# A transformer decoder layer on one core: one table for all eight PSUM banks, and new places for the attention work

## What is computed

```
x = x + attn(layernorm(x))            # self-attention, full 512x512 scores, with biases
x = x + xattn(layernorm(x), ctx_512)  # cross-attention, keys and values from a latent of 128, causal mask
x = x + ffn(layernorm(x))             # 512 -> 2048, exact gelu, -> 512, with biases

scores = einsum('bhsd,bhtd->bhst', q, k) * scale
p = exp(scores - max(scores));  out = (p @ v) / sum(p)
```

## Time and profile before

| | |
|---|---|
| time of the 3 runs, us | 1168.91 (1166.37 to 1170.12) |
| span of the profiled execution, us | 1169.0 |
| mean granted clock of TensorE | 0.996 |
| TensorE busy, us (share) | 1127.7 (96%) |
| TensorE weight loads busy, us | 767.5 (66%) |
| VectorE busy, us | 686.7 (59%) |
| ScalarE busy, us | 485.9 (42%) |
| GpSimd busy, us | 432.9 (37%) |

### The profile page before, as it was taken

How to read it: one execution, slowest core, us unless ns; L and a number is a source line. 1 busy time by engine, 2 the same in 40 slices (tenths; PEclk the granted TensorE clock), 3 DMA queues, 4 the chain that set the end, 5 groups by cost and what they waited for, 6 DMA issues and landing times.

```text
span 1169.0 us, 15851 instructions
## 1 busy us (share of the span) xinstructions
PE 1127.7 (96%) x5840; PEld 767.5 (66%) x5840; DVE 686.7 (59%) x1302; ACT 485.9 (42%) x792; POOL 432.9 (37%) x398
## 2 busy tenths in 40 slices
PE   5999999999999999999999999999999999999998
PEld 4745666656655554665665666657887887887886
DVE  5676767676667667678778777755534214234212
ACT  4365455455555655554645555552221111111110
POOL 1156534443456766445454556663001001001000
PEclk9999999999999999999999999989999999999999
DMA  6933333333334443536345455401210000000000
GB/s 231 291 104 91 108 123 78 109 97 104 91 90 129 138 136 101 165 92 176 103 136 153 127 163 173 115 12 45 90 54 37 1 1 36 0 0 36 1 1 36
DMA packets 73736, 110.29 MB, mean 94 GB/s; under 512 B 6976, under 2 KB 45888, under 8 KB 71744
## 3 DMA queue, kind: packets, MB, share of 16 engines
q1 hardware_dynamic: 70864, 102.00, 29.2%
q0 software_dynamic: 2080, 6.82, 2.2%
q10 hardware_dynamic: 720, 0.54, 0.1%
HBM read 71.58 MB, written 37.75 MB: 94 GB/s over the span
## 4 chain that ended last, share of the span: by engine, by line
PE 86%; DVE 6%; ACT 3%; issue 2%; POOL 2%; DMA 1%; DVEq 0%; ACTq 0%; SPq 0%; POOLq 0%
PE PS L952 18%; PE PS L953 17%; PE PS L954 17%; PE PS L1081 11%; PE PS L1066 10%; PE PS L1047 9%; PE PS L966 1%; ACT PT L871 1%; PE PS L1076 1%; PE PS L1069 1%; POOL P_sum L735 1%; DVE P_sum L1303 1%; DVE PS L1295 1%; ACT stackQ L856 1%; DVE stats L1224 1%
## 5 line engine op out<-in xcount | busy, mean ns | idle before, releaser
L871 ACT ACTIVATE PT<-PS 128x512 f32<-128x512 f32 (+1 forms) x432 | 239.3, 581 | 184.7 <-PE PS L1066 76.6
L735 POOL TENSOR_TENSOR P_sum<-PT 128x512 f32<-128x512 f32 x128 | 161.7, 1283 | 300.8 <-ACT PT L871 300.8
L1289 DVE TENSOR_REDUCE m_cols<-PS 128x1 f32<-128x512 f32 x256 | 171.6, 688 | 77.3 <-PE PS L1047 76.1
L1066 PE MATMUL PS<-stackQ,stackK 100*128 100x512 f32 (+3 forms) x512 | 179.1, 397 | 13.0 <-ACT PT L871 12.2
L1047 PE MATMUL PS<-stackK,stackQ 96*128 96x512 f32 (+3 forms) x512 | 180.5, 389 | 3.1 <-DVE m_cols L1289 1.6
L1376 DVE CAST hidH<-hid 128x512 fp32r<-128x512 f32 x64 | 30.6, 478 | 225.0 <-ACT hid L924 222.9
L924 ACT ACTIVATE hid<-PS,b1c 128x512 f32<-128x512 f32 x64 | 44.1, 690 | 279.9 <-PE PS L954 278.0
L1066 PEld LDWEIGHTS PS<-stackQ,stackK 100*128 100x128 f32 x512 | 92.5, 190 | 91.1 <-ACT PT L871 41.5
L1295 DVE CUSTOM_DVE_ANT_0 PS<-PS,mask_qk 128x128 f32<-128x128 f32 (+3 forms) x256 | 121.2, 512 | 51.6 <-PE PS L1047 50.3
L1303 DVE RECIPROCAL P_sum<-PS 128x512 f32<-128x512 f32 x32 | 107.4, 3358 | 42.5 <-PE PS L1081 42.5
L1047 PEld LDWEIGHTS PS<-stackK,stackQ 96*128 96x128 f32 x512 | 92.2, 191 | 59.8 <-DVE m_cols L1289 22.1
(11 more groups left out here) (124 smaller groups left out, 1769.2 us busy)
## 6 DMA issues: line engine op xcount, KB each, us to landing
scratch<-stage SPq DMA_DIRECT2D x128, 256.0 KB, 2.4
stackK<-scratch SPq DMA_DIRECT2D x62, 256.0 KB, 4.0
stackQ<-scratch SPq DMA_DIRECT2D x46, 256.0 KB, 3.9
stackQ<-scratch SPq DMA_DIRECT2D x18, 512.0 KB, 4.9
stackK<-scratch SPq DMA_DIRECT2D x60, 128.0 KB, 4.6
stackQ<-scratch SPq DMA_DIRECT2D x28, 128.0 KB, 3.8
PT<-wT SPq DMA_DIRECT2D x3, 1024.0 KB, 8.9
x_res<-x SPq DMA_DIRECT2D x3, 1024.0 KB, 8.6
```

The costliest lines, as they stand in the source:

```text
L735: pool.tensor_tensor(P_sum[:, h, :], PT[:, h, :], PT[:, 4 + h, :], ALU.add).then_inc(p_added, 1)
L871: nc.scalar.activation(PT[:, slot:slot + heads, q0:SEQ], PS[:, T_BANK + n % 2, 0:heads * width].rearrange("p (h n) -> p h n", h=heads), AC ...
L1066: mm = nc.tensor.matmul(dst[:, a, :], stackK[0:STACK + HPG, par, h + a, k * P:(k + 1) * P], stackQ[0:STACK + HPG, par, h + a, q0:SEQ], sta ...
L1289: nc.vector.tensor_reduce(m_cols[:, q, STACK + h:STACK + h + heads], bank, AX.X, ALU.max).then_inc(s_done, 1)
```

## The change

1. The fixed banks go. `bank_fills` walks through TensorE's order once, when the program is built, and gives each fill the bank whose last user is free first, by the place of that user plus an estimate from the table FREED of how long its reader takes. It remembers the user before, and `free_bank` waits for exactly that one's reader. Eight banks then serve all kinds together, four of them become the accumulators of the feed-forward part, two those of its transposes, two those of its hidden values.
2. PLACES and the order of the projections in FILL are set anew, and with them the places at which weights are fetched and split (RAW_PLACES, CHUNK_PLACES). The set of instructions that compute is the same: 5840 matmuls of the same shapes.

```diff
-GENERAL = [6, 7]
+BANKS = 8
+FREED = dict(T=0.11, S=0.83, M=2.33, G=1.3, R=4.16, O=5.65)
...
-RAW_PLACES = ((0.0, 1.69, 4.59, 10.14), (16.96, 21.63), (24.23,), (3.78, 24.23, 13.17, 13.33), (13.88,))
+RAW_PLACES = ((0, 0.01, 5.17, 11.56), (14.3, 22.85), (31.55,), (3.64, 24.47, 17.66, 13.33), (13.15,))
...
-                scores=((0.0, 0.6), (2.33, 0.68), (5.8, 1.05), (9.38, 0.98)),
-                values=(5.7, 8.52, 11.43, 17.73),
+                scores=((0.08, 0.7), (2.33, 0.39), (5.66, 1.1), (9.16, 1.52)),
+                values=(4.1, 4.44, 12.02, 17.56),
...
-           (("Wo", 2), "K", ("Wo", 3), "Q"),
-           (("V", 0), "K", ("V", 3), "Q"),
-           (("V", 2), ("V", 1), "Q", "K")),
+           (('Wo', 3), 'Q', ('Wo', 2), 'K'),
+           ('Q', ('V', 0), 'K', ('V', 3)),
+           (('V', 2), 'Q', ('V', 1), 'K')),
...
-BANK = {name: GENERAL[n % 2] for n, name in enumerate(USES)}
...
+def bank_fills():
+
+    fills = [(-2, 0.0, name, True, True) for name in PROLOGUE]
+    fills += [(u, item[0], *fill_of(u, *item[1:])) for u in range(-1, UNITS) for item in PE_ORDER[u]]
+    fills += [(UNITS, 0.0, ("H", i), True, True) for i in (2, 3)]
+    fills += [(UNITS, 1.0, ("Wo", LAST, t), t >= 2, True) for t in range(KT)]
+    bank, before, user, opened, free = {}, {}, {}, set(), {n: (-9, n) for n in range(BANKS)}
+    for u, place, name, opens, closes in fills:
+        if opens:
+            n = min((free[n], n) for n in free if n not in opened)[1]
+            if name[:2] == ("Wo", LAST) and name[2] >= 2:
+                n = bank["Wo", LAST, name[2] - 2]
+            bank[name], before[name], user[n] = n, user.get(n), name
+            opened.add(n)
+        n = bank[name]
+        if closes and name[0] != "H":
+            if name[:2] != ("Wo", LAST):
+                opened.discard(n)
+            later = name[0] in "OR" and u + 1 < UNITS
+            start = (u + 1, PLACES[layer_of(u + 1)][(u + 1) % GROUPS]["divide"]) if later else (u, place)
+            free[n] = (start[0], start[1] + FREED[name[0] if name[0] in FREED else "G"])
...
+            def free_bank(name):
...
+                kind = name[0]
+                if kind == "T":
+                    pe.wait_ge(p_ready, fills_before(name[1]) + name[2] + 1)
+                elif kind == "S":
+                    pe.wait_ge(s_done, fills_before(name[1]) + name[2] + 1)
+                elif kind == "M":
+                    pe.wait_ge(m_copied, 2 * (name[1] + 1))
+                elif kind == "R":
+                    pe.wait_ge(r_done, name[1] + 1)
+                elif kind == "O":
+                    pe.wait_ge(o_done, name[1] + 1)
+                else:
+                    pe.wait_ge(g_done, DONE[name] + 1)
+
             def take_bank(name):
-                n = FULL[name]
-                if n >= 2:
-                    pe.wait_ge(g_done, DONE[USES[n - 2]] + 1)
+                free_bank(BEFORE[name])
...
-                if m >= 2:
-                    pe.wait_ge(p_ready, m - 1)
+                take_bank(("T", u, i))
```

More of the change, by code:

```diff
@@ L122 @@
 CONSTS = 11
-CHUNK_PLACES = [(25, (9.05, 14.91)), (26, (12.2, 12.85)), (28, (7.02, 9.29)), (28, (11.79, 18.46)), (29, (9.87, 17.97)), (30, (12.51, 14.11))]
+CHUNK_PLACES = [(25, (2.12, 13.03)), (26, (5.91, 10.57)), (28, (6.61, 7.41)), (28, (13.83, 14.58)), (29, (10.94, 19.45)), (30, (9.47, 16.47))]
 PLACES = {
-    SELF: (dict(body=22.55,
-                scores=((0.0, 0.6), (2.33, 0.68), (5.8, 1.05), (9.38, 0.98)),
-                values=(5.7, 8.52, 11.43, 17.73),
[L134 to L194, removed]
@@ new lines @@
+    CROSS: (dict(body=22.71,
+                 scores=((0.06, 0.51), (2.49, 0.79), (5.12, 1.59), (8.55, 0.02)),
+                 values=(5.58, 8.61, 8.84, 11.87),
+                 maxima=(5.17, 7.73, 19.33),
+                 fill=(1.83, 10.03, 22.33),
+                 stats=7.39,
+                 divide=2.71,
+                 output=4.29),
+            dict(body=27.59,
+                 scores=((0.07, 0.37), (2.29, 0.38), (5.5, 1.11), (7.82, 0.7)),
+                 values=(3.5, 5.38, 11.23, 11.6),
+                 maxima=(2.14, 5.48, 13.28),
+                 fill=(-2.83, 7.99, 14.02),
+                 stats=-5.83,
+                 divide=-3.2,
+                 output=3.13),
+            dict(body=14.89,
+                 scores=((0, 0.25), (1.66, 0.61), (6.12, 0.97), (9.01, 0.57)),
+                 values=(5.23, 5.63, 10.4, 12.22),
+                 maxima=(3.42, 6.65, 8.52),
+                 fill=(1.35, 5.99, 9.99),
+                 stats=17.22,
+                 divide=-2.08,
+                 output=4.37),
+            dict(body=22.49,
+                 scores=((0.31, 0.49), (3.27, 0.7), (5.81, 1.22), (9.1, 0.38)),
+                 values=(4.96, 6.56, 15.58, 16.03),
+                 maxima=(2.51, 9.81, 11.74),
+                 fill=(7.67, 9.22, 15.73),
+                 stats=4.37,
+                 divide=0.39,
+                 output=5.79)),
@@ L274, in pe_order @@
     assert not any(item[1:3] == ("Wo", 0) for item in work) or g == 0
+    for item in work:
+        pieces = [other[3] for other in work if other[1:3] == item[1:3]]
+        assert pieces == sorted(pieces)
     assert "xT" not in kinds or not {"Q", "K"} & set(kinds[kinds.index("xT"):])
@@ L382, in last_of, with fill_of @@
     return last
-BANK = {name: GENERAL[n % 2] for n, name in enumerate(USES)}
+def fill_of(u, what, which, piece):
+    if what == "scores":
+        return ("T", u, which), True, True
+    if what == "max":
+        return ("S", u + 1, which), True, True
+    if what == "turn":
+        return ("M", which), True, True
+    if what == "values":
+        return ("O", u), which == 0, which == KT - 1
+    if what == "sums":
+        return ("R", u), True, True
+    if what == "up":
+        return ("H", which), piece == 0, piece == KT - 1
+    if what == "partial":
+        return ("Wo", LAST, which), piece == 0, False
+    return use_of(u, what, which, piece)
+def bank_fills():
[18 more added lines that the diff above has]
+            free[n] = (start[0], start[1] + FREED[name[0] if name[0] in FREED else "G"])
+    acc = [bank["H", i] for i in range(FIRST_UPS)]
+    turned = [bank["Wo", LAST, t] for t in (0, 1)]
+    hidden = [n for n in range(BANKS) if n not in acc + turned]
+    assert len(hidden) == 2
+    return bank, before, acc, turned, hidden, [user.get(n) for n in hidden]
+BANK, BEFORE, ACC_BANKS, F_BANKS, H_BANKS, H_BEFORE = bank_fills()
 def decoder_layer(nc, x, ctxT, wT, bq, bk, bv, bo, wq2T, wkv2T, wo2T, p1T, b1, p2T, b2, out, scratch):
@@ L542, in H @@
             first = isinstance(b, int) and b == 0 and i < FIRST_UPS
-            return PS[:, ACC_BANK + i if first else H_BANK + i % 2, :]
+            return PS[:, BANK["H", i] if first else H_BANKS[i % 2], :]
         def fraw(i):
@@ L1286, in maximum @@
                 dve.wait_ge(s_full, m + 1)
-                bank = PS[:, S_BANK + m % 2, 0:heads * n].rearrange("p (h n) -> p h n", h=heads)
+                bank = PS[:, BANK["S", u, i], 0:heads * n].rearrange("p (h n) -> p h n", h=heads)
                 if layer_of(u) == SELF:
```

92 lines of the change are left out of this document (59 added, 33 removed).

## The result

The change took **1128.94 us** (median of 4 runs, 1127.77 to 1130.39) against 1169.32 us in the same comparison: a ratio of 0.966, 95% interval 0.9645 to 0.9673. The profiled execution spans 1128.2 us.

What follows compares the result with a forecast made beforehand. TensorE's stream, busy 96% of 1169.0 us, was taken to set the time. Terms -10.5 (a), -6.3 (b), -2.1 (c), +3 (d) and nothing for (e) sum to -15.9, so 1153 us; 8 in 10 range 1137 to 1167 us.

Steps and rivals of the forecast that it cites:

- (a): TensorE's 23 long bank waits of the scores behind ScalarE's exp: two thirds won, -10.5 us, between 0 and -16.1.
- (b): Short bank waits of T loads for the exp and S loads for VectorE: half won, -6.3 us, between 0 and -12.6.
- (c): Fewer changes between value blocks and other matmuls on TensorE, 123 runs of blocks instead of 129: -2.1 us.
- (d): New waits because the banks of O and R now go to other fills early, before VectorE has read them: +3 us.
- R3: Rival: R's bank is taken too early, TensorE waits behind a late reciprocal in each unit's first 6 us: 1176 us, chance 0.09.
- (e): Moved K and Q projections, their stores and stack loads on SP, and raw-weight splits on POOL: cost nothing.
- R1: Rival: the bank waits only move, for instance to the value blocks, no change: 1166 us, chance 0.13.
- R2: Rival: the freed banks are used fully, all of (a) to (c) won and the slow stretch gone: 1138 us, chance 0.20.
- R4: Rival: TensorE's clock swings, a slow stretch at each start of a cross unit: +48 us, 1201 us, chance 0.01.
- the clock: TensorE's one stretch at 1.2 GHz may vanish if pauses shrink: up to -3 us, not in the sum.

Runs made afterwards that it cites:

- e2: The change with PLACES, FILL, RAW_PLACES and CHUNK_PLACES of before, so old order with the new table of banks: 1164.6 us, ratio 0.998.
- e7: The change with all numbers of FREED set to 0: 1182.8 us, ratio 1.0098.
- e3: The change, but O and R keep a bank each (4 and 5) and all other kinds share the other six: 1144.6 us, ratio 0.9796.
- e5: e2 with one number of FREED changed, G=1.3 to G=2.5 (when a projection's bank counts as free): 1159.0 us, ratio 0.9925.
- e9: e2 with the eight `stats=` places (layer norm's statistics) taken from the change: 1153.2 us, ratio 0.9873.
- e10: The change with the eight `stats=` places (layer norm's statistics) of before: 1134.7 us, ratio 0.9705.
- e11: The change with RAW_PLACES and CHUNK_PLACES of before (fetching and splitting of raw weights): 1130.6 us, ratio 0.967.
- e1: The change with its new places and fills, but the fixed banks of before: 1247.4 us, ratio 1.067.

## Why the prediction was wrong

**What bounds the kernel: right.** TensorE's stream sets the time, the gain lies between 50 and 800 us, in every part of it, and what follows unit 31's row sums did not move (374.7 and 374.8 us).

**(a) and (b), the bank waits: right in kind, far too small.** To size them again I took, for each matmul, the time from the start of the one before, less the tenth percentile of that time, in the same profile, for the same two kinds and sizes. This excess holds whatever delays a start, not bank waits alone. Summed from 37 us to the row sums of unit 31 it falls as follows:

| excess in front of | before, us | after, us |
|---|---|---|
| the third T of a unit | 12.9 | 1.7 |
| the fourth T | 3.0 | 0.2 |
| other T | 18.8 | 8.4 |
| S | 15.8 | 9.9 |
| projections | 26.2 | 18.7 |
| masks | 5.7 | 4.0 |

That is 39.5 us. Of it 30.3 us are of T and S, which I had put at 16.8 in the sum and at 28.7 at most; 9.2 us stood in front of projections and masks, to which I had given no term. In units 1 to 15 of e2, where the order is that of before and only the banks differ, the excess of T, S and projections falls by 14.7 us, of the 15.5 us by which these units are shorter; so there it measures the bank waits.

Two errors made my terms so small. First, the fraction: "I take two thirds" and "I take half" had the waits come back at the value blocks; of such waits the profile after has one, of 0.2 us, on line 1139. Second, the size. I added up waits that the views list, and took 107.16 busy us of 107.90 as a sign that steady units have nearly nothing to give. The modelled end of a row lies 0.17 us beyond the next start, so a shorter wait disappears inside "busy". e2 measures it, since its order is that of before. The start of unit 6, before and in e2:

```profile
210.10 0.73 PE L1066 MATMUL PS<-stackQ,stackK 100*128 100x512 f32 x2
...
211.46 0.89 PE L1066 MATMUL PS<-stackQ,stackK 100*128 100x512 f32 x2
...
215.55 0.39 PE L1066 MATMUL PS<-stackQ,stackK 100*128 100x512 f32 x1
```

```profile
206.00 0.73 PE L1123 MATMUL PS<-stackQ,stackK 100*128 100x512 f32 x2
207.25 0.62 PE L1123 MATMUL PS<-stackQ,stackK 100*128 100x512 f32 x2
...
210.75 0.39 PE L1123 MATMUL PS<-stackQ,stackK 100*128 100x512 f32 x1
```

The same eight T and four sets of projections take 5.45 us before and 4.75 us with free banks. That is 0.70 us in one unit, of which not one row of TensorE's own waits speaks: four steps between a T and its neighbour are longer, by 0.10 to 0.27 us each. I had priced one of them (0.15 us) and counted only those that the loads' view lists.

**(c), merged value blocks: not contradicted.** By the same measure the excess of the whole program, all kinds included, fell by 38.5 us; that leaves 2.3 of the 40.8 us between the two profiled executions for structure, against 2.1 forecast. No run isolates it.

So the way from the 15.9 us of the sum to 40.8 is: 13.5 more for T and S, 9.2 for projections and masks, 3.0 for the new waits of (d), which did not come, 0.2 for (c), and 1.0 back for all other kinds and the start.

**(d) and R3, the early reuse of O's and R's banks: the mechanism is real, the change avoids it.** The sum had +3 us; the profile after has no wait on the reciprocal or the product among TensorE's (e2 has seven, 3.8 us). e7 takes the estimates away and gets 30 us of such waits and 1182.8 us, in the direction and near the size of the rival (1176 us), though part of its loss is the clock. e3, which excludes it, is not faster but 16 us slower. What I had not seen is that the places of VectorE's work matter as much as the bank that is chosen (e5 against e9, and e10).

**(e), moved projections, loads and splits: right as far as the profile shows.** No wait of TensorE there names a transfer, and behind unit 0 the longest is 1.4 us, behind ScalarE, and e11 puts the raw weights' places at 1.6 us.

**R1** (the waits only move) is what e2 looks like in its total, 1164.6 us against 1166 forecast, but not for its reason: there real gains of 15.5 us were eaten by VectorE's queue in the cross units. **R2** (all waits gone, 1138 us) was the right story with the smaller price list, and I had given it 0.20 because I expected the order to be limited by ScalarE's exps. Seven exps in 3.72 us show ScalarE without a gap, and T goes on all the same: with banks enough it need not wait for each exp. **R4** did not come: between 22.7 us and the last 3 us no stretch at the lower clock is left. In the Trainium skill's case of bank cycling (TensorE: Matmul & The Clock Gate, "A second HAM failure mode: psum-queue depth-cycling") brief pauses made the clock swing; e1, with 69 waits of T alone, has six stretches at the lower level and a mean clock of 0.988, so the trace agrees with the rule that far. The sharing of banks does not do it by itself: e2 and the change share all eight, e2 has three such stretches, each behind a wait of 3.5 us, and the change none.

## What to carry to other kernels

Where an engine is "busy" over 95%, compare the start-to-start times of its rows with its pace on the same kinds of rows: waits shorter than the modelled overlap add up, and no view of waits lists them in full; here TensorE's listed waits for banks were some 15 us, the gain 40. Buffers given out "free first" and the order of the queues that read them belong together: the freed banks gave 3 us under the old order, the new order lost 80 us (some 70 without the flaw at the start) without the banks, and both won 40. And look at how such a table breaks ties: fills with the same place all got the same bank, which cost 8 to 10 us in three experiments. With an engine that works in order, a wrong guess costs all that is queued ahead of the reader, so look first at what is queued ahead of the reader, and move that, before choosing another buffer.

## What the runs showed of the hardware

A pause of TensorE of a few microseconds can cost more than itself. In e2 the windows around the wait of unit 19, columns as in the earlier trace rows:

```profile
526.60:530.57 3.97, 0.48 (x5) 0.28 (x4) 3.93 (x19) 1.00 (x3) 3.97 (x4) 1.00 0.00 0
530.57:534.20 3.63, 3.63 (x19) 1.10 (x20) 0.72 (x4) 0.00 (x0) 1.40 (x2) 0.53 0.72 223
```

After 0.48 busy us of 3.97 the clock is at its lower level (1.2 GHz) for nearly all of the next window, and two value blocks take 3.05 us (530.57 to 533.62) where 1.85 is their time at the full clock (216.11 to 217.96): 1.2 us more on top of 3.5. e7, with some 30 us of waits behind VectorE, has twelve stretches at the lower level and a mean clock of 0.980; the change, without them, has 0.999. I had put the clock aside with at most 3 us, which holds for the change (0.996 to 0.999 is some 3.5 us, an estimate from the mean clocks and 1169 us), but it makes versions with long waits worse than their waits alone.
